# Sixteen-head cross-attention in a fused two-layer kernel: one reduction for the row maxima of both head groups

## The reference

```python
qh = jnp.einsum('bshd,hed->bshe', q, wq) + bq
kh = jnp.einsum('bthd,hed->bthe', kv, wk) + bk
vh = jnp.einsum('bthd,hed->bthe', kv, wv) + bv
scores = jnp.einsum('bshd,bthd->bhst', qh, kh) / jnp.sqrt(d)
attn = jax.nn.softmax(scores, axis=-1)
ctx = jnp.einsum('bhst,bthd->bshd', attn, vh)
out = ctx.reshape(b, sq, e) @ wo.T + bo
```

## Time and profile before

| what | value |
|---|---|
| median of 3 runs | 1964.88 us (1962.65 to 1965.19) |
| the profiled execution | 1961.54 us, its span 1959.7 us |
| TensorE busy over the span | 1763.4 us (90%) |
| VectorE | 1072.6 us (55%) |
| ScalarE | 855.4 us (44%) |
| GpSimd | 642.7 us (33%) |
| L1026, row maxima | 512 instructions, 192.1 us, 415 ns each |
| L725, exponentials | 512 instructions, 238.6 us, 472 ns each; idle before them 237.5 us |
| granted TensorE clock | 0.955 mean, 0.99 from 100 to 1320 us |

### The profile page before, as it was taken

The page is one execution under the profiler, slowest core; times in us unless marked ns, Lnnn a source line. Parts: engine busy times, 40 slices in busy tenths (PEclk is TensorE's granted clock), DMA queues, the critical chain, the costliest instruction groups (busy, mean ns, idle before and its releaser), DMA issues. The chain is left out here.

```text
span 1959.7 us, 43596 instructions
## 1 busy us (share of the span) xinstructions
PE 1763.4 (90%) x12680; PEld 1443.3 (74%) x12713; DVE 1072.6 (55%) x3790; ACT 855.4 (44%) x2361; POOL 642.7 (33%) x1186
## 2 busy tenths in 40 slices
PE   3799999999999999999999999883599999999990
PEld 2477777767776776777777777762599999999990
DVE  4567766767676776776777777766311111111115
ACT  0466655656565665665665666641111111111110
POOL 0234333433343333433343334330133333333320
PEclk7899999999999999999999999995699999999996
DMA  9522322222222222222222221005544555455547
GB/s 326 209 74 86 97 66 80 86 79 85 78 87 78 89 75 83 83 87 76 82 82 85 80 82 37 6 12 204 186 173 178 187 185 175 177 185 184 179 146 263
DMA packets 124402, 235.82 MB, mean 120 GB/s; under 512 B 14448, under 2 KB 76400, under 8 KB 114096
## 3 DMA queue, kind: packets, MB, share of 16 engines
q1 hardware_dynamic: 117392, 214.87, 32.9%
q0 software_dynamic: 6816, 18.62, 2.5%
HBM read 203.16 MB, written 30.28 MB: 119 GB/s over the span
## 5 line engine op out<-in xcount | busy, mean ns | idle before, releaser
L725 ACT ACTIVATE x_prob<-ps,x_nmax 128x257 f32<-128x257 f32 x512 | 238.6, 472 | 237.5 <-DVE x_nmax L1026 237.1
L1413 ACT ACTIVATE heT<-ps 128x512 f32<-128x512 f32 x142 | 84.8, 597 | 441.3 <-PE ps L1379 441.3
L447 PE MATMUL ps<-context,x_probT 128*128 128x128 f32 x2048 | 275.4, 278 | 0.9 <-ACT x_probT L719 0.8
L1379 PEld LDWEIGHTS ps<-xeT,w_block 128*128 128x128 f32 x2272 | 266.2, 193 | 12.8 <-issue 8.5
L1379 PE MATMUL ps<-xeT,w_block 128*128 128x128 f32 x2272 | 266.9, 276 | 8.6 <-DMA w_block<-in_m_w 8.1
L447 PEld LDWEIGHTS ps<-context,x_probT 128*128 128x128 f32 x2048 | 259.6, 194 | 10.7 <-issue 2.5
L1365 PE MATMUL ps<-w,heT 128*128 x1136 | 256.8, 379 | 0.0
L1365 PEld LDWEIGHTS ps<-w,heT 128*128 128x128 f32 x1136 | 210.4, 190 | 25.7
L1026 DVE TENSOR_REDUCE x_nmax<-ps 128x1 f32<-128x257 f32 x512 | 192.1, 415 | 40.2 <-PE ps L612 40.2
L719 ACT ACTIVATE x_probT<-ps 128x512 f32<-128x512 f32 x224 | 133.7, 597 | 146.0 <-PE ps L606 142.9
L790 POOL TENSOR_TENSOR x_lastv<-context,x_prob 128x128 f32<-128x128 f32 x256 | 120.4, 470 | 227.3 <-ACT x_prob L725 227.3
(11 more groups left out here) (269 smaller groups left out, 3131.1 us busy)
## 6 DMA issues: line engine op xcount, KB each, us to landing
w_block<-in_m_w SPq DMA_DIRECT2D x71, 1024.0 KB, 4.8
context<-in_cT SPq DMA_DIRECT2D x128, 257.0 KB, 2.9
context<-in_cn SPq DMA_DIRECT2D x128, 256.0 KB, 3.0
context<-in_lastk SPq DMA_DIRECT2D x128, 128.0 KB, 3.6
yrows<-zero SPq DMA_DIRECT2D x1, 8192.0 KB, 30.3
w<-in_m_w SPq DMA_DIRECT2D x8, 1024.0 KB, 12.5
w<-yrows SPq DMA_DIRECT2D x16, 512.0 KB, 6.0
xin<-in_x SPq DMA_DIRECT2D x32, 128.0 KB, 3.1
```

Source lines behind the costliest of these rows:

```text
L447: t = mm(out, a, b, start=n == 0, stop=n == len(pairs) - 1)
L725: A(p1[kk % 2][:, g, :], ps[:, g, 0:KEYS], ACT.Exp, bias=nmax1[kk % 2][:, g:g + 1], accum_out=rsum1[kk % 2][:, g:g + 1]).then_inc(e1_ok.ha ...
L1379: t = mm(ps[:, 2 * b + n, f * P:(f + 1) * P], w1[b][:, k, lo:lo + P], xeT[b][:, k, :], start=k == 0, stop=k == H - 1)
L1413: A(heT[b][:, n * FK // 2:(n + 1) * FK // 2, :].rearrange("p k t -> p (k t)"), ps[:, 2 * b + n, :], ACT.Gelu).then_inc(heT_ok.handle, 1)
```

## The change

The two reductions of a half unit become one that reads both banks, 2 x 257 columns, and still gives two maxima, one per group, since it reduces along the last axis alone. It waits for the scores of both groups, and both exponentials wait for it. The signal `m1_ok` counts one step per half unit in place of two. TensorE's, GpSimd's and SyncE's lists are the same; VectorE's has 256 reductions fewer; ScalarE's has one wait in place of two ahead of each pair of exponentials.

```diff
-    s1_ps, m1_ok, e1_ok = sig("x1_scores_in_psum", 2), sig("x1_row_max", 2), sig("x1_probs", 2)
+    s1_ps, m1_ok, e1_ok = sig("x1_scores_in_psum", 2), sig("x1_row_max", 1), sig("x1_probs", 2)
...
                         t, m, kk, K = sl.half(k)
+                        W(act, m1_ok, K, 1)
                         for g in (0, 1):
-                            W(act, m1_ok, K, g + 1)
                             A(p1[kk % 2][:, g, :], ps[:, g, 0:KEYS], ACT.Exp, bias=nmax1[kk % 2][:, g:g + 1], accum_out=rsum1[kk % 2][:, g:g + 1]).then_inc(e1_ok.handle, 1)
...
             def unit_max(t, m, k, K):
-                for g in (0, 1):
-                    W(dve, s1_ps, K, g + 1)
-                    v_.tensor_reduce(nmax1[k % 2][:, g:g + 1], ps[:, g, 0:KEYS], AX, ALU.max, negate=True).then_inc(m1_ok.handle, 1)
+                W(dve, s1_ps, K, 2)
+                v_.tensor_reduce(nmax1[k % 2][:], ps[:, 0:2, 0:KEYS], AX, ALU.max, negate=True).then_inc(m1_ok.handle, 1)
```

## The result

The changed kernel is slower. Its median is 1979.34 us (1977.54 to 1984.3) against 1964.74 us (1962.65 to 1965.19) in the same session; the ratio is 1.008, with a 95% interval from 1.0061 to 1.01. That is 14.6 us more, where 27.8 were forecast; the direction and the range held, the size did not. The profiled execution took 1977.54 us, with a span of 1975.5.

What follows compares the result with a forecast made beforehand. TensorE was taken to bound the stage, with no slack on the path scores, maximum, exponential, transpose. Terms A to E summed to 27.8 us on 1964.9, so 1992.7 us, range 1976 to 2008.

Steps and rivals of the forecast that it cites:

- (a): Every half unit: the first exponential waits for the maximum of both groups, so both exponentials come 0.27 us later.
- (b): Where VectorE waits for TensorE: the reduction also waits for group 1's scores, starting 0.21 us later; exponentials 0.48 later in all.
- A: k = 4: the transposes of the probabilities wait 0.48 us longer in each of 32 tiles, 15.4 us.
- B: k = 2: ScalarE's later self_normT makes the next query product wait 0.25 us in each of 32 tiles, 8.0 us.
- C: k = 0 and 1: 0.27 us later transposes, partly absorbed, leave 0.15 in 24 slots; 3.0 us in all.
- D: k = 3, 5, 6, 7: enough cover, or at k = 6 a loss of 1.6 against a gain of 1.7; about 0.
- E: Last tile, without another layer's work as cover: k = 0, 6 and 7 pay 0.48 us each, 1.4 us.
- R1: Rival, chance 0.07: VectorE's chain decides at k = 1 and 6, so the kernel gains 4.5 us, to 1960.4.
- R2: Rival, chance 0.06: TensorE makes the lost time up, no change, 1965 us, a few either way.
- R3: Rival, chance 0.20: only A counts, the ScalarE shifts of B and C vanish in queue order; 15 us more, 1980.
- R4: Rival, chance 0.07: the joined reduction takes 0.83 us, so more half units wait; 45 us more, 2010.

Runs made afterwards that it cites:

- parted kernels: The kernel before plus a 128-row product between the two groups' scores at k = 4: 2001.81 us with one reduction there, 1985.22 with two.
- dve_both: The kernel before, but VectorE waits for both groups' scores ahead of the first of its two reductions; ScalarE waits as before: 1962.58 us, 0.9996.
- the kernel with the fill: The kernel before with one reduction at k = 4 alone and a one-column VectorE fill in place of the second reduction: 1967.31 us, 1.002.
- only4: The kernel before with one reduction for both groups at k = 4 alone, two everywhere else, no fill: 1980.16 us, 1.0096.

## Why the prediction came out as it did

**The bound, and where it gives way: right.** TensorE is the bound, VectorE's saved time bought nothing, and the path scores, maximum, exponential, transposes was the one that mattered.

**The reduction: right.** 0.68 us forecast, 687 ns measured; 0.66 to 0.83 was the range.

**(a) 0.27 us on every exponential: right.** At k = 0, where VectorE comes late, it is 0.27 exactly: the step went from 2.94 to 3.21.

**(b) 0.21 us more where VectorE waits for TensorE: wrong, 0.04 to 0.05.** This is the step that failed, and it is what made the forecast almost twice the measured loss; the direction and the range held in spite of it. I took four matmul records in two pairs to be group 0, then group 1, because the code issues them so. The `64*128` in the same rows said that each fills half the array. The parted kernels show that the groups ran side by side. All terms built on 0.48 are too large:

| term | forecast, us | measured in the steps |
|---|---|---|
| A, k = 4 | 0.48 x 32 = 15.4 | 0.31 x 32 = 9.9 |
| B, k = 2 | 0.25 x 32 = 8.0 | 0.07 x 32 = 2.2 |
| C, k = 0 and 1 | 0.15 a plain slot, 3.0 | 0.27 - 0.12 = 0.15 a plain slot; 3.7 outside the loop turns |
| D, the others | about 0 | k = 6 gains 0.15 in one slot of four, k = 5 changes little: -1.0 |
| E, the last tiles | 1.4 | 93.2 instead of 90.9 us from tile 29 on; of these 2.3, 1.2 are not in A and B |
| six loop turns | -0.6, within C, for eight | +1.5 in this execution |
| sum | 27.8 | 17.5 |

The first scores begin 0.9 us earlier in the changed kernel's execution, so the stage ends 16.6 later; the span grew by 15.8, the median by 14.6. The loop turns once per four slots, six times in the stage, and not in eight of 32 slots as term C has it; that is worth under 1 us.

A and B fell by 5.5 and 5.8 us, 11.3 of the 13.2 by which the forecast of the loss was too large, and B lost most of its size: it was 0.48 less a slack of 0.23 us, and 0.31 less the same slack is 0.08. E was small for another reason: each place pays 0.27 to 0.31 and not 0.48, but tile 30 pays as well as tile 31. A term that is a small difference between a shift and a slack carries the shift's whole error.

B after the change, the rows that answer to the earlier trace rows: self_normT ends at 690.72 and the loads of its product follow at 690.77, the 0.05 of a hand-over later. Counted from the start of the scores of k = 2 that is 3.37 us, before 3.29: the wait is there, 0.08 long.

```profile
690.32 0.40 ACT L660 ACTIVATE self_normT<-ps 128x256 f32<-128x256 f32 x1
690.37 0.60 PE L606 MATMUL ps<-constants,x_prob 128*128 128x128 f32 x4
...
690.77 0.52 PEld L447 LDWEIGHTS ps<-self_normT,w_a_Wq 128*128 128x128 f32 x4
```

**C, the absorption by k = 1: the sum right, one step on the way wrong.** In microseconds from the start of the slot, the product with `x_W` was to come 0.10 later. It starts at 5.68, before at 5.71: 0.03 earlier. The copy L1039 (before L1040) is 0.18 later, as forecast. But `cross_norm` behind it takes VectorE 0.40 us instead of 0.55, so that the reduction of k = 1 starts at 4.72, before at 4.69, and the shorter reduction gives 0.06 back. TensorE's own delay goes into its wait for `self_norm` (L455), which was 0.20 us before and is gone. What makes the 0.15 is the other path, and that came as forecast: ScalarE carries the 0.27 through the gelu to self_normT, which ends at 7.97 (before 7.70), and the loads behind it start at 8.02 (before 7.87).

```profile
680.68 0.20 PEld L606 LDWEIGHTS ps<-constants,x_prob 128*128 128x128 f32 x2 [0.25 <-ACT x_prob L725]
...
682.56 0.68 DVE L1025 TENSOR_REDUCE x_nmax<-ps 128x2 f32<-128x514 f32 x1
...
683.52 1.10 PE L447 MATMUL ps<-x_W,x_outT 128*128 128x256 f32 x4 [0.39 <-DVE x_outT L1030]
...
685.43 0.38 ACT L660 ACTIVATE self_normT<-ps 128x256 f32<-128x256 f32 x1
...
685.86 0.30 PEld L447 LDWEIGHTS ps<-self_normT,w_a_Wq_T 128*128 128x128 f32 x2
```

The wait of 0.25 in the first row is the 0.27 that k = 0 pays, as C had it for the earlier trace rows.

**D: the one slot in four went the other way.** I had 0.20 us lost at its k = 6 against 0.07 gained; it gained 0.15. TensorE's wait for `x_norm` there is 0.41 us, before 0.50. But dve_both has the same 0.41 and the same 3.89 with two full reductions, so this is the stall of VectorE in the kernel before that went away, not the shorter reduction. Nothing in the prediction foresaw it.

**The rivals.** R1 (VectorE's chain decides) fell with the steps at k = 4. Something of its mechanism may live in the kernel that joins only where cover exists, which is 2.7 us below the kernel before; k = 1, where R1 has it, is 0.04 to 0.06 shorter there. R2 (TensorE makes the time up) is true for 3 us at most of what k = 4 costs, by the kernel with the fill. R3 (only A) is nearest to the time, 1980 for 1979.34, by luck: it has A at 15 and nothing else, and the steps have A at 9.9, B at 2.2 and C at 3.7. R4 did not come. The rule against the change (the Trainium skill, Perfetto Trace Analysis, Optimizing Scalar/DVE Operations: break instructions up where the engine is not saturated but leaves bubbles elsewhere) agrees with the result, 14.6 us slower when two became one. It speaks of whole engines, and VectorE is not saturated in this stage; that a pair can be joined at five places of eight without loss is this case's own finding.

**Left open.** What makes one instruction of VectorE take 0.86 us in one slot of four (only4) or 0.45 with 0.37 us of standing ahead of it (the kernel before), and why the loop turns differ by some microseconds between the profiled executions, was not settled. By the steps of one profiled execution each kernel is known to some 0.01 us a step, but the turns of the loop (from 1.3 us shorter to 5.3 longer in sum than before) blur its total.

## What to carry to other kernels

Joining two instructions saves the joining engine some 0.07 us here and delays the first consumer by the second half, 0.27 us. So ask at each place who is late: where the engine itself comes late and its consumer has cover, join; where the consumer waits, leave the pair split. In an unrolled schedule that answer differs from unit to unit, and joining in five of eight was 1% better than in all and 0.1 to 0.2% better than in none, the latter not shown to come from the joining. And before a delay is read off a merged row of matmuls, look at the form: here products on half the array ran as pairs.

## What the hardware showed that I had not expected

- Two products of 64 rows on different halves of the array take 0.70 us together, and one takes 0.70 alone; a product of 128 rows between them puts the second 1.04 us behind the first.
- A busy TensorE share rose from 37.24 to 37.91 us in a slot with the same matmuls: a wait inside a merged group is partly shown as work.
- With one instruction of VectorE fewer per tile (only4), one masking of every fourth slot took 0.86 us instead of 0.29. That cost 0.6 us in the three slots where TensorE's granted clock stayed at 1.00, and 2.1 to 2.3 in the four where it was 0.57 to 0.66 for some four microseconds, after 1.1 us of standing. A comparison of two schedules can carry this; the fill tells it apart.
- The kernel before has a smaller stall of the same engine, 0.15 us at k = 6 in one slot in four, that a kernel with the same instructions and one wait changed (dve_both) has not.
